# Second attention of a two-layer transformer step: a third score bank, values weighted for two key tiles in a row, and projections moved to other heads

## The reference, cut to what matters

```python
q = input_tensor @ wq.T + bq
k = input_tensor @ wk.T + bk_
v = input_tensor @ wv.T + bv
# split in 16 heads of 16
scores = jnp.einsum('bhsd,bhtd->bhst', q, k) / jnp.sqrt(jnp.float32(D))
attn = jax.nn.softmax(scores, axis=-1)
out = jnp.einsum('bhst,bhtd->bhsd', attn, v)
return out.reshape(B, S, E) @ wo.T + bo
```

## Time and profile before

| | |
|---|---|
| three executions, median | 1987.37 us (1984.23 to 1990.66) |
| profiled execution | 1987.64 us |
| its span in the trace | 1985.8 us |
| TensorE busy / VectorE busy / ScalarE busy | 93% / 71% / 60% of the span |
| second attention | 1398.6 us to the end |
| reduce to maxima (L1584), in all | 338.4 us, 512 of 686 ns |
| exponentials (L1677), in all | 290.2 us |
| scores (L1463) / transposed scores (L1472) | 237.1 / 207.0 us |
| `weigh` (L1482) | 135.8 us, 1024 instructions of 604 ns |

### The profile page before, as it was taken

One profiled execution on the slowest core, in us unless ns is written; L12 is line 12 of the kernel. 1 busy time (PEld: TensorE's weight loads), 2 busy tenths in 40 slices (PEclk: granted clock), 3 DMA queues, 4 the chain that ended last, 5 costly groups with the idle time before them and its releaser, 6 DMA issues. The chain is left out here.

```text
span 1985.8 us, 32448 instructions
## 1 busy us (share of the span) xinstructions
PE 1847.7 (93%) x11568; PEld 1411.5 (71%) x11568; DVE 1411.8 (71%) x2881; ACT 1191.2 (60%) x2809; POOL 605.4 (30%) x958
## 2 busy tenths in 40 slices
PE   1999999999999999999999959998799999999997
PEld 1887888878778888878888758887455555555553
DVE  5785885885885867858858854443677777777773
ACT  3665675674664765756756755554466666666664
POOL 0354353443543443543534523222100110011012
PEclk9999999999999999999999989999799999999999
DMA  6111111211111111111101157332733444353421
GB/s 234 42 34 33 44 43 27 49 44 33 43 33 44 41 25 46 41 33 43 44 25 41 43 170 286 120 115 74 202 106 101 133 146 120 112 163 93 132 70 43
DMA packets 104047, 162.34 MB, mean 82 GB/s; under 512 B 11984, under 2 KB 53456, under 8 KB 103376
## 3 DMA queue, kind: packets, MB, share of 16 engines
q1 hardware_dynamic: 103368, 159.75, 28.1%
q10 hardware_dynamic: 520, 0.52, 0.1%
HBM read 80.55 MB, written 46.14 MB: 64 GB/s over the span
## 5 line engine op out<-in xcount | busy, mean ns | idle before, releaser
L1584 DVE TENSOR_REDUCE nm<-ps 128x1 f32<-128x512 f32 x512 | 338.4, 686 | 120.3 <-PE ps L1463 117.6
L1677 ACT ACTIVATE pt<-pst 128x512 f32<-128x512 f32 x512 | 290.2, 599 | 194.1 <-PE pst L1472 191.6
L805 POOL TENSOR_SCALAR pr<-pr,rinv 128x128 f32<-128x128 f32 (+3 forms) x512 | 263.2, 533 | 374.8 <-DVE rinv L693 374.8
L573 ACT ACTIVATE pr<-sc,nmax 128x128 f32<-128x128 f32 (+3 forms) x512 | 268.1, 527 | 143.4 <-DVE nmax L682 141.9
L682 DVE TENSOR_REDUCE nmax<-sc 128x1 f32<-128x128 f32 (+3 forms) x512 | 223.3, 485 | 76.5 <-PE sc L409 76.4
L1463 PE MATMUL ps<-kb,qb 96*128 96x512 f32 x512 | 237.1, 465 | 27.5 <-DMA kb<-z_scratch 15.3
L811 POOL TENSOR_TENSOR qk<-ra,rb 128x256 f32<-128x256 f32 x256 | 182.9, 735 | 206.4 <-DVE rb L704 170.9
L1463 PEld LDWEIGHTS ps<-kb,qb 96*128 96x128 f32 x512 | 97.9, 191 | 185.5 <-DVE nm L1584 123.6
L1472 PE MATMUL pst<-qb,kb 128*128 128x512 f32 x512 | 207.0, 406 | 3.4 <-ACT pt L1677 2.9
L421 PE MATMUL w<-ident,pr 128*128 128x128 f32 x1280 | 170.6, 280 | 25.7 <-DVE rb L704 19.8
L1419 POOL TENSOR_TENSOR so<-so,g_sb 128x256 f32<-128x256 f32 x32 | 23.5, 733 | 535.4 <-DVE so L1621 535.4
(11 more groups left out here) (213 smaller groups left out, 4227.6 us busy)
## 6 DMA issues: line engine op xcount, KB each, us to landing
k<-k SPq DMA_DIRECT2D x256, 128.0 KB, 2.2
z_scratch<-zt SPq DMA_DIRECT2D x96, 256.0 KB, 2.5
qb<-z_scratch SPq DMA_DIRECT2D x64, 192.0 KB, 3.8
kb<-z_scratch SPq DMA_DIRECT2D x64, 192.0 KB, 4.0
raw<-in_w SPq DMA_DIRECT2D x16, 640.0 KB, 6.1
raw<-in_w SPq DMA_DIRECT2D x8, 704.0 KB, 4.2
xa<-in_x SPq DMA_DIRECT2D x2, 2048.0 KB, 13.8
x<-in_x SPq DMA_DIRECT2D x8, 512.0 KB, 4.0
```

The costliest lines, as they stand in the source:

```text
L573: act.activation(pr[:, h, SOFF[i]:SOFF[i] + (i + 1) * P], sc[:, bank, at:at + (i + 1) * P], ACT.Exp, bias=nmax[:, h, i:i + 1], accum_out=r ...
L805: pool.tensor_scalar(p, p, rinv[:, h, i:i + 1], 1.0, ALU.mult, ALU.mult).then_inc(scaled, 1)
L1584: dve.tensor_reduce(nm[:, g % 2, i, h:h + 1], ps[:, i % 2, :], AXX, ALU.max, negate=True).then_inc(max_done, 1)
L1677: act.activation(pt[:, g % 2, h, i, :], pst[:, i % 2, :], ACT.Exp).then_inc(exp_done, 1)
```

## The change

`ps` gets a third bank, and tile n = 16q + 4h + i uses bank n % 3; `score` waits for the maximum of tile n - 3. The bank `pn` is gone: `turn_n` writes to bank 0 or 1 of `w` by the table `NBANK`, `turn_o` always to bank 0, and both wait for what was last in that bank to have been read, as do the steps that use the bank after them. `weigh` is called twice in a row at the ends of heads 1 and 3 (key tiles 0 and 1, then 2 and 3), not once at the end of each head. The tables `V_PE`, `V_DVE`, `O_PE` and `O_DVE` put the values' and the output's projections in heads 0 and 2; `Z_PE` stays.

```diff
@@ -1291,10 +1291,9 @@
         on = t.sb("on", [P, NT, C])
         ot_hi, ot_lo = (t.sb(n, [P, NC, T], F32R) for n in ("ot_hi", "ot_lo"))
         so = t.sb("so1", [P, 2, C])
-        ps = t.ps("ps", [P, 2, 512])
+        ps = t.ps("ps", [P, 3, 512])
         pst = t.ps("pst", [P, 2, 512])
         po = t.ps("po1", [P, 512])
-        pn = t.ps("pn", [P, 512])
         w = t.ps("w1a", [P, 2, 512])
         sn_hi_done = t.sem("a_sn_hi_done")
         xs_in = [t.sem(f"a_xs_in{r}") for r in range(2)]
@@ -1333,9 +1332,11 @@
 
 
 
+        NBANK = (0, 0, 1, 0)
+
         Z_PE, Z_ACT, Z_DVE = ((0, 2), (2, 0)), ((0, 3), (2, 1)), ((1, 1), (2, 2))
-        V_PE, V_DVE = ((1, 0), (1, 3), (2, 1), (2, 3)), ((1, 1), (2, 0), (2, 2), (3, 0))
-        O_PE, O_DVE = ((0, 2), (1, 1), (2, 0), (2, 3)), ((0, 3), (1, 2), (2, 1), (3, 0))
+        V_PE, V_DVE = ((0, 1), (0, 3), (2, 1), (2, 3)), ((0, 2), (1, 0), (2, 2), (3, 0))
+        O_PE, O_DVE = ((0, 1), (0, 3), (2, 0), (2, 2)), ((0, 2), (1, 0), (2, 1), (2, 3))
 
         with nc.Block() as block:
             @block.sync
@@ -1444,6 +1445,8 @@
                 def project_v(b, i):
                     if i > 1:
                         pe.wait_ge(vn_done, NT * b + i - 1)
+                        if i == 2 and b > 1:
+                            pe.wait_ge(on_done, NG1 * (b - 1))
                     elif b > 0:
                         pe.wait_ge(c.zt_lo_done, 4 * b + i + 1)
                     else:
@@ -1459,8 +1462,9 @@
                     if h == 0 and i == 0:
                         pe.wait_ge(stack_in[g], 64 * (q // NG1) + 64)
                     n = 16 * q + 4 * h + i
-                    pe.wait_ge(max_done, n)
-                    pe.matmul(ps[:, i % 2, :], qb[0:2 * S3, g, h // 2, i * P:(i + 1) * P], kb[0:2 * S3, g, h, :],
+                    if n > 2:
+                        pe.wait_ge(max_done, n - 1)
+                    pe.matmul(ps[:, n % 3, :], qb[0:2 * S3, g, h // 2, i * P:(i + 1) * P], kb[0:2 * S3, g, h, :],
                               start=True, stop=True).then_inc(s_done, 1)
 
                 def score_t(q, g, h, i):
@@ -1485,19 +1489,40 @@
                         mm.then_inc(av_done, 1)
 
                 def turn_n(q):
+                    b, g = q // NG1, q % NG1
                     pe.wait_ge(sn_done, q + 1)
-                    if not isinstance(q, int) or q > 3:
+                    if q > 3:
                         pe.wait_ge(on_done, q - 2)
-                    for i in range(NT):
-                        mm = pe.transpose(pn[:, i * P:(i + 1) * P], sn[:, i].rearrange("p a b -> p (a b)").bitcast(F32), c.ident[:])
+
+                    if g == 2 and b < B - 1:
+                        pe.wait_ge(vn_done, NT * (b + 1) + NT)
+                    elif g == 2:
+                        pe.wait_ge(so_done, NT * (b - 2) + NT)
+                    elif q == 0:
+                        pe.wait_ge(c.zt_lo_done, 3)
+                    elif g == 0 and b > 1:
+                        pe.wait_ge(so_done, NT * (b - 2) + 3)
+                    elif g % 2 and b < B - 1:
+                        pe.wait_ge(c.zt_lo_done, 2 * (2 * (b + 1) + g // 2) + 1)
+                    for i in range(NT):
+                        mm = pe.transpose(w[:, NBANK[g], i * P:(i + 1) * P], sn[:, i].rearrange("p a b -> p (a b)").bitcast(F32), c.ident[:])
                     mm.then_inc(n_turned, 1)
 
                 def turn_o(q, n_turns):
+                    b, g = (q + 2) // NG1, (q + 2) % NG1
                     pe.wait_ge(ou_done, q + 1)
                     pe.wait_ge(n_dve, n_turns)
                     pe.wait_ge(n_act, n_turns)
-                    for i in range(NT):
-                        mm = pe.transpose(pn[:, i * P:(i + 1) * P], ou[:, i * P:(i + 1) * P], c.ident[:])
+                    if b < B - 1 and g % 2 == 0:
+                        pe.wait_ge(c.zt_lo_done, 2 * (2 * (b + 1) + g // 2) + 1)
+                    elif b < B - 1 and g == 1:
+                        pe.wait_ge(vn_done, NT * (b + 1) + 1)
+                    elif b == B:
+                        pe.wait_ge(so_done, NT * (B - 2) + 3)
+                    elif g == 3 and b > 0:
+                        pe.wait_ge(so_done, NT * (b - 1) + 1)
+                    for i in range(NT):
+                        mm = pe.transpose(w[:, 0, i * P:(i + 1) * P], ou[:, i * P:(i + 1) * P], c.ident[:])
                     mm.then_inc(o_turned, 1)
 
                 def turn_on(b, k):
@@ -1507,6 +1532,9 @@
                         pe.wait_ge(vn_done, NT * (b + 2) + NT // 2 + k + 1)
                     else:
                         pe.wait_ge(so_done, NT * (b - 1) + NT // 2 + k + 1)
+                    if k == 1 and b < B - 1:
+                        pe.wait_ge(n_dve, NG1 * b + NG1 + 3)
+                        pe.wait_ge(n_act, NG1 * b + NG1 + 3)
                     for i in range(NT):
                         mm = pe.transpose(w[:, k, i * P:(i + 1) * P], on[:, i, k * P:(k + 1) * P], c.ident[:])
                     mm.then_inc(on_turned, 1)
@@ -1518,6 +1546,8 @@
                             pe.wait_ge(c.zt_lo_done, 4 * (b + 2) + 2 + i + 1)
                     else:
                         pe.wait_ge(so_done, NT * b + i - 1)
+                        if i == 2 and b < B - 1:
+                            pe.wait_ge(on_done, NG1 * (b + 1) + 2)
                     for k in range(NC):
                         oh, ol = (a[:, k, i * P:(i + 1) * P] for a in (ot_hi, ot_lo))
                         pe.matmul(w[:, i % 2, 0:C], oh, wo_hi[:, k, :], start=(k == 0), stop=False)
@@ -1548,8 +1578,10 @@
                                 turn_n(q + 1)
                             if h == HG - 1 and g == 1 and not first and i >= 2:
                                 turn_on(b - 1, i - 2)
-                        if back1:
-                            weigh(q - 1, (g + 3) % NG1, h, b + 1 if g else b)
+
+                        if back1 and h % 2:
+                            for kt in (h - 1, h):
+                                weigh(q - 1, (g + 3) % NG1, kt, b + 1 if g else b)
 
                 for n in range(HG + 1):
                     for i in range(NT):
@@ -1580,8 +1612,9 @@
                 def maximum(q, g, h, i):
                     if h == 0 and i == 0 and not (isinstance(q, int) and q < 2):
                         dve.wait_ge(sn_done, q - 1)
-                    dve.wait_ge(s_done, 16 * q + 4 * h + i + 1)
-                    dve.tensor_reduce(nm[:, g % 2, i, h:h + 1], ps[:, i % 2, :], AXX, ALU.max, negate=True).then_inc(max_done, 1)
+                    n = 16 * q + 4 * h + i
+                    dve.wait_ge(s_done, n + 1)
+                    dve.tensor_reduce(nm[:, g % 2, i, h:h + 1], ps[:, n % 3, :], AXX, ALU.max, negate=True).then_inc(max_done, 1)
 
                 def split_n(q, g):
 
@@ -1594,12 +1627,12 @@
 
                 def take_n(q, g):
                     dve.wait_ge(n_turned, q + 1)
-                    dve.tensor_copy(qb[2 * S3:P, g, 0, :], pn[0:2 * D1, :]).then_inc(n_dve, 1)
+                    dve.tensor_copy(qb[2 * S3:P, g, 0, :], w[0:2 * D1, NBANK[g], :]).then_inc(n_dve, 1)
 
                 def take_o(q, g):
 
                     dve.wait_ge(o_turned, q + 1)
-                    v = pn[:].rearrange("p (t h d) -> p t h d", t=NT, h=HG)
+                    v = w[:, 0, :].rearrange("p (t h d) -> p t h d", t=NT, h=HG)
                     dve.reciprocal(inv[:], v[:, :, :, D1:D1 + 1]).then_inc(inv_done, 1)
                     dve.wait_ge(inv_done, q + 1)
                     dve.tensor_tensor(on[:, :, g * HG * D1:(g + 1) * HG * D1].rearrange("p t (h d) -> p t h d", h=HG),
@@ -1678,7 +1711,7 @@
 
                 def take_n(q, g):
                     act.wait_ge(n_turned, q + 1)
-                    act.copy(qb[2 * S3:P, g, 1, :], pn[2 * D1:4 * D1, :]).then_inc(n_act, 1)
+                    act.copy(qb[2 * S3:P, g, 1, :], w[2 * D1:4 * D1, NBANK[g], :]).then_inc(n_act, 1)
 
                 def take_o(q):
                     act.wait_ge(av_done, q + 1)
```

## The result

The changed kernel takes 1993.05 us (median of 20 executions, 1989.79 to 1994.52) against 1988.57 (20 of the kernel before): a ratio of 1.0024, interval 1.0018 to 1.0029. It is slower by a quarter of a per cent: clear of noise, and less than the 0.3% within which I had called it the same. The profiled execution takes 1992.76, its span is 1991.0.

What follows compares the result with a forecast made beforehand. TensorE, busy 93%, was taken as the bound, with only its waits to win. Batches 1 to 6 +4.0, last -2.4, first -1.1, fill -0.3: +0.2 on 1987.64, forecast 1988 us, range 1973 to 2000.

Steps and rivals of the forecast that it cites:

- the likeliest case: Whole kernel: the time laid out by hand from the timeline's steps holds, 1983 to 1993 us, chance 0.50.
- 0.34 for `turn_n` behind the split: Fourth group: `turn_n` waits 0.34 us behind the split, within a group forecast at 16.1, from 17.12.
- The steps of an even group: First group, from its first score: head 2 at 9.24, `rest_z` 12.96, `turn_n` 14.87, next group at 18.2 us.
- the chain: All groups: engine steps and waits laid from one even group's timeline, good to about 0.15 us a group.
- Double calls: Ends of heads 1 and 3: two `weigh` calls together take 2.06 us in place of 2.40, saving 0.68 a group.
- with the double calls worth nothing, 21 is added: Upper bound: without the saving of 0.68 us in each of 31 groups, 21 is added, giving 2009.
- Wait one: Even groups, head 1 after tile 2: `turn_o` waits for `rest_z` of bank 0 and goes at 6.27 us.
- Second group: Odd group forecast at 17.75 us, from 18.08, with `turn_n` in bank 1 waiting 0.98 for `take_v` of tile (3, 0).
- First and last batch: Outside batches 1 to 6: the first batch gains 1.1 us and the last batch 2.4.
- Rival A: Score banks: the third bank decouples TensorE and VectorE, so the kernel is faster, 1975 us; chance 0.27.
- Rival B: Behind each turn: 2.06 us blocks starve VectorE and ScalarE, 13 odd groups lose 0.7 each, 1997 us; chance 0.19.
- Rival C: Ends of heads 1 and 3: a double `weigh` call costs as much as two single ones, 2009 us; chance 0.04.

Runs made afterwards that it cites:

- x4_out_late: The changed kernel with VectorE's last `take_out` moved back from tile (2,3) to (3,0): 1989.28 us, ratio 0.9999.
- x14_mixed: x10_all_single with double `weigh` calls in odd groups and in the last batch only: 1968.0 us, ratio 0.9892 to the kernel before.
- x2_double: The kernel before with the double `weigh` calls alone (two score banks, turns in `pn`, old projection places): 1997.45 us, ratio 1.0042.
- x1_single: The changed kernel with one `weigh` call at the end of every head again, all else kept: 1986.43 us, ratio 0.9989.
- x3_double_tables: The kernel before with double `weigh` calls and the new projection places, still two score banks and turns in `pn`: 1994.3 us, ratio 1.0026.
- x5_turn_bank: The changed kernel with `turn_o` in bank 1 in even groups, so that it no longer waits for `rest_z`: 1986.0 us, ratio 0.9990.
- x8_v_early: The changed kernel with the values' last two projections at (2,0) and (2,2), taken at (2,1) and (2,3): 1990.02 us, ratio 1.0008.
- x12_two_banks: x10_all_single with two score banks and the turns in `pn`: 1983.82 us, ratio 0.9974 to the kernel before.
- x10_all_single: The changed kernel with single `weigh` calls, `turn_o` in bank 1 in even groups, values' last projections early and last `take_out` late: 1972.52 us, ratio 0.9920.
- x13_z_late: The changed kernel with the second projection of even groups one tile later, (2,1) in place of (2,0): 1989.65 us, ratio 1.0006.

## Why the prediction held, point by point

- *The number.* 1988 was forecast, 1983 to 1993 for the likeliest case alone, and "within 0.3%". Measured: +0.24%, 5 us over the number, at that case's upper edge. In batches 1 to 6 +4.0 was forecast and +8.6 came, so 4.6 of the 5 us are there.
- *The groups.* 18.2, 17.75, 18.4 and 16.1 were forecast; 18.20, 17.84, 18.53 and 16.62 came. Three of four are within 0.13. The step that failed is the fourth group's "0.34 for `turn_n` behind the split": the split was taken at 0.18 for its subtraction, and it is 0.72. The move of `take_out` to (2,3) released GpSimd's multiply onto it. I had followed that move on VectorE and TensorE, and not to GpSimd, which the working leaves out. Six times 0.52 is 3.1 of the 4.6 us. x4_out_late shows it: 15.97 without it.
- *The steps of an even group.* From the group's first score, head 2 was forecast at 9.24, its second score at 11.1, `rest_z` at 12.96 and `turn_n` at 14.87; the trace has 9.15, 11.12, 13.00 and 14.83 (1565.40, 1567.37, 1569.25 and 1571.08). So the chain was right, and not only its sum. The steps written down for its end add up to 18.29, though, not to the 18.2 that was put.
- *Double calls.* 2.06 in place of 2.40: the run at 1563.55 gives 1565.40 - 1563.55 + 0.11 + 0.10 = 2.06, and x14_mixed shows the 0.34. That they lose in even groups what they save and more is shown by x2_double (18.20 with two banks) and by x1_single. The bound "with the double calls worth nothing, 21 is added" was wrong in sign: with single calls 7 us go away. It counts the saved instructions in full, while the chain beside it had the even groups lose by the same blocks.
- *Wait one.* Forecast at 6.27 after the group's first score, measured at 1562.53 - 1556.25 = 6.28. But its share in the loss was not told apart by my sum: the even groups lose 1.0 with it or without it, since the kernel with two banks pays as much in waits of scores for maxima (x3_double_tables). They get there by different heads (3.71, 5.10, 3.84 and 5.55 in x3_double_tables, 3.62, 5.54, 3.62 and 5.42 here), so that the sums agree looks like chance. Mending it gives 0.41 and 0.47 (x5_turn_bank).
- *Second group.* The wait of `turn_n` for `take_v` was forecast at 0.98 idle; 0.8 was measured, the group came 0.1 longer than forecast, and taking the wait away gave 0.4 (x8_v_early).
- *First and last batch.* -1.1 and -2.4 forecast, -2.0 and -1.7 measured.
- *What the profile would show.* The double `weigh` was forecast at 1.93 and took 1.92; TensorE's idle before `turn_o` in even groups, up to 0.5, was 0.24; before `turn_n`, 0.6 and more, it was 0.34, 0.81 and 0.54 in the first, second and fourth group.
- *Rival A* (the banks decouple, 0.27) was wrong as built, and right in small: mended, the bank gives some 10 us. The rule of the Trainium skill that a repeating gap can mean too little PSUM (Perfetto Trace Analysis, Identifying Performance Opportunities) is borne out by x12_two_banks against x10_all_single, 11 us. As built, the gap moved to the next semaphore, since the turns had been moved into another stage's banks.
- *Rival B* (0.19) was wrong in its place: the odd groups did not lose. But its sign, the fourth group not under 16.6, did come up (16.62), by a cause that nobody had named: with the blocks in place and GpSimd's multiply elsewhere the group takes 15.97. The blocks have a share in it, as the held subtraction costs nothing with single calls. *Rival C* is refuted by the run of 16.

What stays open: how the double call's price in even groups divides beyond the quarter of x13_z_late; and why the second group with single calls and three banks (17.5) stays 0.7 over the 16.8 of TensorE's own work there, after the mending; nothing was run on `turn_on` alone.

## What to carry to other kernels

A wait table names what an engine waits for, not what it would gain: 68 us in 400 of waits for a bank went away and the stretch grew, as the next semaphore held TensorE instead. Look first at what the bottleneck itself lost: here 0.9 us of idle time for the banks and some 14 us of open weight loads. Merging short calls saves their change-over (0.34 us here), but each was also the cover under which slower engines caught up. Here the merged calls paid in the odd groups and cost 0.9 in the even ones, so try them group by group. When a step moves, follow what its result releases on every engine, GpSimd too.

## What the runs showed of the hardware

A small VectorE instruction with two operands in SBUF was held while a GpSimd multiply ran: the subtraction took 0.72 us in the six of its 32 executions that GpSimd's multiply met, and 0.18 otherwise. The copy with one operand was held as well: in the kernel before it took 0.42 to 0.43 in the same six places, and there nobody waited for it. The Trainium skill (SBUF — State Buffer, Who interferes with whom) has it so for two operands: the two engines share a port pair that one holds for a whole instruction, and a VectorE operation with two SBUF inputs blocks until a GpSimd one that reads SBUF is through. The trace agrees: the subtraction ended 0.03 us after the multiply.
